# Where side jobs of an attention kernel begin, who reads them in its tail, and the order of its first rows

## The chip, the core and the metric

The kernel runs on one NeuronCore of a Trainium2 chip. The metric is the device time of one execution in microseconds (us). PE is TensorE, DVE is VectorE, ACT is ScalarE, POOL is GpSimd and SP is SyncE, which here issues most of the DMAs.

## What is computed

The input x has 4 batches of 1024 rows of 128 features. All of it is float32. Two blocks with a layer norm ahead follow each other, both with 16 heads of 8 features.

```python
x = x + attention(layernorm(x))      # softmax over (q k / sqrt(8)) * tril(k=-1), then @ Wr + br
x = x + ffn(layernorm(x))
# ffn(y): q, k from rotary(y), v from y; causal attention, out projection
#   x1 = layer_norm(y + attn_out)
#   gates = softmax(x1 @ gate_w.T + gate_b), the two largest of 8 experts
#   moe = sum of the two experts' outputs (x1 @ expert_w + expert_b) times their gates
#   return layer_norm(x1 + moe)
```

In the first attention the scores above the diagonal are multiplied by zero ahead of the softmax, so they still count in its sum. In the second they are minus infinity.

## The kernel before

**Slots and sets.** There are 8 attentions, 4 batches of 2 blocks, and each is a *slot* (`SLOTS`). Their order mixes the blocks: (0,0), (0,1), (1,0), (0,2), (1,1), (0,3), (1,2), (1,3). A slot has 8 passes (half of the queries, 4 heads), and a pass goes through *sets* of key tiles (`SETS`), 3 for the first half of the queries and 7 for the second. So a slot has 40 sets and all slots have 320. A full set has two *units*. A unit is one ACTIVATE, the exponential over 128x1024 scores (line 1275). The last set of each pass is a half set with one unit. There are 576 units.

**What the engines do for a set g.** PE writes the scores (`scores_set`, line 1101). It may begin when the first exponential of set g-1 has been taken, since there are three pairs of PSUM banks for scores. ACT takes the exponentials, POOL masks the diagonal tiles (line 1351), and PE multiplies the probabilities of set g-3 with the values (`value_group`, line 1130, `LAG` is 3). Once a pass, ACT copies the sums out of PSUM (`evacuate`, line 1218).

**Side jobs.** All other work of PE (projections, transposes, the gates, two jobs e0 and e1 for each tile of 128 rows with the eight experts) is cut into *jobs*, 219 in all, of which 178 stand beside the sets. Each writes one bank, `side`, and DVE reads it out before the next may begin. For one attention of the second block, work `p2` makes q, k and v ahead of it, and work `p3` is what follows it. `p1` makes them for the first block. Everything else that is not attention is a *turn* of DVE, POOL, ACT or SP.

**Who sets the order.** `schedule()` runs while the kernel is built. It keeps a clock for each engine and writes down what each engine does at each of 640 points, two to a set. Point 2g lies between the scores of set g and the values of set g-3, and point 2g+1 after those values. Every job and turn has a latest time, from `ends` and `UNIT_TIME`. Before the change a job may begin when `credit` is above zero. That is an account which fills evenly with what is left to do, and from which each job takes its PE time, so jobs are spread evenly whatever PE and ACT are at. What is left after set 319 stands in `AFTER`, the tail. Each engine works its list in order and waits on semaphores. In the tail the six score banks serve as job banks as well.

**The tail.** The last half of the rows is `LAST_HALF`, rows 512 to 1023 of batch 3 in the second block. After its attention come `num` (transposes of the sums), `att`, `att_turned`, `out`, `stats`, `root`, `centre`, `scale`, `x1T`, `gate`, `exp`, `pick0` to `pick3`, `GT`, `bias`, the four tiles' `e0`, `e1` and `moe`, then `stats2`, `root2`, `centre2`, `scale2` and `store`. For a tile DVE multiplies the two banks of e0 and e1 with the gates (`prod`, line 1391) and adds the two (`psum`), and POOL adds the rest (`moe`, lines 1332 to 1334).

**The start.** `BEFORE_TURNS` is written by hand. DVE first works on `pairs`, a small bound made from the weights, for which PE waits for `first_weights_in`. Five loads count on that semaphore, `bv` the last of them.

## Time and profile before

| what | value |
|---|---|
| median of 3 runs | 813.0 us (808.07 to 815.91) |
| the profiled execution | 811.53 us |
| its span, first to last instruction | 809.8 us |
| mean granted clock of TensorE | 0.938 |
| first exponential begins | 32.04 us |
| last store issued, landed | 806.51 us, 809.32 us |
| PE, ACT, DVE, POOL busy | 660.4, 632.5, 409.4, 323.6 us |

The profile is of one execution, and its span is 1.7 us shorter than that execution's time. The kernel has three stretches: a start of 32 us without exponentials, the 320 sets, and a tail after the last exponential, which begins at 745.66 us and takes 1.11 us. An idle time in the rows is that of the engine just before the instruction, and the arrow names what ended it.

### The profile page before, as it was taken

The page shows a single profiled execution, that of the slowest core. Times are in us where ns is not written, and L with a number is a line of the kernel's source. Part 1 is how long each engine was busy: PE and PEld are TensorE (multiplying, and loading weights), DVE is VectorE, ACT ScalarE, POOL GpSimd, SP SyncE. Part 2 cuts the span into 40 slices and gives each one's busy share as a digit, 9 for nine tenths or more (in the row PEclk, how much of TensorE's full clock was granted, in tenths as well). Part 3 has the DMA queues.
Part 4 walks back from the last instruction along what each step waited for, and adds up shares of the span by engine and source line. Part 5 has one row for each costly group of instructions (what it writes and reads, how often), then busy time and mean ns, then how long its engine had stood idle before and what let it go on. Part 6 is the DMA issues. An engine that isn't in the chain of part 4 may idle for free. (4 is left out here: it accounts for less than half of the span.)

```text
span 809.8 us, 15314 instructions
## 1 busy us (share of the span) xinstructions
PE 660.4 (82%) x5560; PEld 246.2 (30%) x5560; DVE 409.4 (51%) x1115; ACT 632.5 (78%) x665; POOL 323.6 (40%) x635
## 2 busy tenths in 40 slices
PE   3589888898798879879878889899888889799643
PEld 2324223332233223223223323323322323223321
DVE  4365452355354542564444634553734535545876
ACT  1389998899799987889979899798898997977000
POOL 3162245332532433534643436414743346224323
PEclk9699999999899998999989999889999999999857
DMA  5866467363566343433365334241554434410000
GB/s 136 272 203 207 146 218 227 99 203 134 185 231 188 134 141 98 133 93 118 121 210 159 132 106 147 81 132 49 170 193 145 158 96 121 119 53 2 26 26 15
DMA packets 76992, 109.78 MB, mean 136 GB/s; under 512 B 13784, under 2 KB 28256, under 8 KB 76896
## 3 DMA queue, kind: packets, MB, share of 16 engines
q1 hardware_dynamic: 73232, 107.85, 42.0%
q10 hardware_dynamic: 3664, 0.77, 0.5%
q8 instruction: 46, 0.75, 0.4%
q14 instruction: 50, 0.41, 0.2%
HBM read 60.91 MB, written 47.68 MB: 134 GB/s over the span
## 5 line engine op out<-in xcount | busy, mean ns | idle before, releaser
L1275 ACT ACTIVATE probs<-scores,shift 128x1024 f32<-128x1024 f32 x576 | 600.7, 1124 | 101.6 <-PE scores L1101 96.1
L1351 POOL TENSOR_SCALAR_AFFINE_SELECT probs<-probs 128x256 f32<-128x256 f32 (+1 forms) x448 | 197.9, 460 | 393.6 <-ACT probs L1275 392.5
L1130 PE MATMUL acc<-probs,v 128*9 128x512 f32 (+3 forms) x3072 | 326.5, 514 | 0.9 <-ACT num L1218 0.8
L1101 PE MATMUL scores<-qs,ks 32*128 32x512 f32 (+3 forms) x1536 | 161.2, 435 | 81.0 <-ACT probs L1275 78.9
L1101 PEld LDWEIGHTS scores<-qs,ks 32*128 32x128 f32 x1536 | 72.9, 189 | 282.4 <-ACT probs L1275 200.6
L1130 PEld LDWEIGHTS acc<-probs,v 128*9 128x9 f32 x3072 | 59.0, 101 | 109.8 <-issue 71.7
L1391 DVE TENSOR_TENSOR prod<-side,G 128x512 f32<-128x512 f32 x47 | 32.5, 691 | 85.2 <-PE side L1083 75.0
L1083 PE MATMUL side<-we,x1T 128*128 128x512 f32 x94 | 54.5, 663 | 3.6 <-DVE shift L1521 2.0
L1218 ACT ACTIVATE num<-acc 128x512 f32<-128x512 f32 x64 | 38.3, 599 | 5.8 <-PE scores L1005 3.3
L1332 POOL TENSOR_TENSOR moe<-psum 128x256 f32<-128x256 f32 x32 | 23.9, 747 | 42.6 <-DVE x1b L1391 25.4
L1307 POOL TENSOR_TENSOR rstd<-rstd,expo 128x4 f32<-128x4 f32 x32 | 33.8, 1056 | 2.7
L1240 ACT ACTIVATE ga<-gl 128x32 f32<-128x32 f32 x8 | 2.0, 246 | 31.5 <-DVE gl L1391 31.5
L1391 DVE TENSOR_TENSOR psum<-prod 128x512 f32<-128x512 f32 x32 | 23.4, 732 | 4.7 <-POOL y L1334 0.6
L1424 DVE COPY xT<-side 128x512 f32<-128x512 f32 x22 | 15.1, 686 | 18.4 <-PE side L956 18.4
L1436 DVE TENSOR_SCALAR part<-side,binqk 128x512 fp32r<-128x512 f32 x16 | 12.0, 749 | 23.0 <-PE side L962 21.3
L1083 PEld LDWEIGHTS side<-we,x1T 128*128 128x128 f32 x94 | 14.3, 191 | 28.0 <-issue 12.4
L1306 POOL TENSOR_SCALAR rstd<-mv 128x4 f32<-128x4 f32 x32 | 8.0, 250 | 33.5 <-DVE mv L1402 33.5
L1406 DVE TENSOR_SCALAR xn<-xrow,mv,rstd 128x128 f32<-128x128 f32 x32 | 11.2, 410 | 19.0 <-POOL rstd L1307 19.0
L1083 PE MATMUL scores<-we,x1T 128*128 128x512 f32 x34 | 20.3, 713 | 0.0
L1436 DVE TENSOR_SCALAR part<-side,bqk 128x512 fp32r<-128x512 f32 x12 | 9.0, 751 | 20.5 <-PE side L962 20.5
L1399 DVE BATCH_NORM_STATS2 stats<-xrow 128x6 f32<-128x128 f32 x64 | 13.8, 276 | 10.6 <-DMA xrow<-in_x 7.5
L962 PE MATMUL side<-xT,win 128*128 128x512 f32 x32 | 18.0, 645 | 0.0
(171 smaller groups left out, 604.3 us busy)
## 6 DMA issues: line engine op xcount, KB each, us to landing
ks<-k_dram SPq DMA_DIRECT2D x96, 256.0 KB, 4.0
q_dram<-part SPq DMA_DIRECT2D x64, 256.0 KB, 3.1
qs<-q_dram SPq DMA_DIRECT2D x64, 256.0 KB, 3.1
num_dram<-num SPq DMA_DIRECT2D x60, 256.0 KB, 3.3
k_dram<-part SPq DMA_DIRECT2D x32, 256.0 KB, 3.6
xrow<-in_x SPq DMA_DIRECT2D x16, 256.0 KB, 4.3
nat<-num_dram SPq DMA_DIRECT2D x15, 256.0 KB
rdenb<-rden_dram SPq DMA_DIRECT2D x15, 256.0 KB
```

Of the source, the lines that this page charges most:

```text
L962: signal(pe.matmul(out[:, :], w[:, int(name == "k"), :], xT[a][:, a or j, :], start=True, stop=True), last)
L1083: signal(pe.matmul(out[:, :], x1T[i // TH][:, i % TH, :], we[:, first:first + HALF], start=True, stop=True), last)
L1101: ins = pe.matmul(scores[:, pair(g, h // 2), h % 2, col:col + w], ks[u][r, kt // TH, (kt % TH) * P:(kt % TH + 1) * P], qs[u][r, q0:q0 + w] ...
L1130: ins = pe.matmul(acc[h * VW:h * VW + VC, q0:q0 + w], v9[V_OF[k]][:, kt, :, HG * hg + h], src, start=(s == 0), stop=last, skip_group_check ...
L1218: act.activation(num[gp % 2][:, :], acc[:, :], ACT.Copy).then_inc(acc_read, 1)
L1275: act.activation(dst, src, ACT.Exp, bias=shift[:, column(k):column(k) + 1], scale=SCALE).then_inc(probs_raw, 1)
L1307: pool.tensor_tensor(r, r, expo[:, 0:1].broadcast_to(list(r.shape)), ALU.pow).then_inc(root_ready[w], 1)
L1332: link(pool.tensor_tensor(moe[:, :, :], psum4[:, i % 2, 0:2, :], psum4[:, i % 2, 2:4, :], ALU.add))
L1351: ins = pool.affine_select(out=blocks, in_=blocks, compare_op=ALU.is_ge, fill=0.0, base=a - 1, pattern=[[0, blocks.shape[1]], [1, P]], cha ...
L1391: return dve.tensor_tensor(out, in0, in1, op)
L1424: freeing(dve.tensor_copy(xT[a][:, int(name == "rT") if a else j, :], written(job)))
L1436: link(dve.tensor_scalar(pt[:, c, 0, :], src, bias[:, c:c + 1], None, ALU.add))
```

## The change

There are four parts. All of them change the lists of the engines, three by the plan and one by new instructions.

**Where jobs begin.** `credit` is gone. A job may begin when, by the build's clocks, PE would be at most `LATE` (0.5) behind the earliest time of its next scores after the job. Jobs of `p2` are free of that rule, and so is any job whose latest time has passed. The clocks' numbers change, and `UNIT_TIME` goes from 1.25 to 1.15.

**The tail's plan.** It now orders by the longest way left (`left`) and plans PE and DVE apart. 37 jobs are in the tail and 29 were.

**Who reads the tail's banks.** In the tail ACT multiplies the products of all e1 jobs and of the e0 jobs of other halves than the last, 19 of 23, with four ACTIVATEs of 128x128 each. It also copies `x1T` and `GT` (2 each, where their job is in the tail) and `att_turned`. DVE no longer does these, but waits at their place in its list and counts the bank free (`read_by_act`). Products of the tail go to the buffers of `probs`. The last half has its own tiles for y, x1 and x2 (`y_of`, `x1_of`, `x2_of`), in `xrow0` and `xrow`, so it need not wait for the halves before it.

**The start.** The rows' statistics come ahead of `pairs`, `xT` ahead of `bound`, `bv` has its own semaphore, ACT makes the first part of k for both halves (`K_BY_ACT`), and ACT issues the two DMAs of the first k instead of SP.

```diff
+def by_act(x):
+    return x[2] in ("e1", "x1T", "GT", "att_turned") or (x[2] == "e0" and (x[1], x[3] // TH) != LAST_HALF[1:])
...
-BEFORE_TURNS = ([("p0", 0, "pairs", 0), ("p1", 0, "stats", 0), ("p1", 0, "stats", 1), ("p1", 0, "root", 0), ("p1", 0, "root", 1),
-                 ("p1", 0, "rows", 0), ("p0", 0, "bound", 0), ("p1", 0, "rows", 1), ("p1", 0, "xT", 0), ("p0", 0, "roots", 0),
+BEFORE_TURNS = ([("p1", 0, "stats", 0), ("p1", 0, "root", 0), ("p1", 0, "stats", 1), ("p1", 0, "root", 1), ("p0", 0, "pairs", 0),
+                 ("p1", 0, "rows", 0), ("p1", 0, "xT", 0), ("p0", 0, "bound", 0), ("p1", 0, "rows", 1), ("p0", 0, "roots", 0),
...
-UNIT_TIME = 1.25
+UNIT_TIME = 1.15
+LATE = 0.5
...
-        credit = min(credit + side_left / (NPOINT - p), 1.5)
         room = p % 2 or len(units) > 1
-        if room and open_job is None and banks[-1] <= t and credit > 0 and p + 4 < NPOINT:
-            x = next((x for x in pending if x[2] in PIECES and ready(x, t, p)), None)
+        if room and open_job is None and banks[-1] <= t and p + 4 < NPOINT:
+            ahead = t + (0.49 * len(UNITS_OF[g - LAG]) if p % 2 == 0 and g >= LAG else 0.0) - exps[FIRST_UNIT[g]] - 0.1
+            x = next((x for x in pending if x[2] in PIECES and ready(x, t, p)
+                      and (x[0] == "p2" or ahead + JOB_TIMES[x[2]][0] * JOB_TIMES[x[2]][1] <= LATE or late(x) < t)), None)
...
+        if clock["DVE"] <= t:
+            x = next((x for x in pending if x[2] not in PIECES and turn_time(x)[0] == "DVE" and ready(x, t, NPOINT)), None)
+            if begun and begun[0][1] <= t and ready(begun[0][0], t, NPOINT) and (x is None or left(begun[0][0]) > left(x)):
+                x, _end = begun.pop(0)
...
-        n_first = len(FIRST) + 1
+        n_first = len(FIRST)
...
+        def k_out(engine, a, b, j):
+            engine.wait_ge(side_free, done((("p1", "p2")[a], b, "k", j)))
+            use = part_count(a, b, j)
+            for d in range(2):
+                engine.dma_start(k_d[a][b, j, :, :, d].rearrange("h e s -> (h e) s"),
+                                 part[use % 2][:, 1, d, :].bitcast(F32)).then_inc(part_out[use % 2], 16)
...
+                if (work, b, name, i) in K_BY_ACT:
+                    act.wait_ge(side_done, done((work, b, name, i)))
+                    act.activation(part[part_count(0, b, i) % 2][:, 1, 0, :], bank_of((work, b, name, i)), ACT.Identity, bias=bqk[:, 1:2]).then_inc(act_parts, 1)
+                if (work, b, name, i) == ("p1", 0, "parts_out", 0):
+                    k_out(act, 0, b, i)
...
+                if job in BY_ACT:
+                    act.wait_ge(side_done, done(job))
+                    src = bank_of(job)
+                    if name in ("e0", "e1"):
+                        act.wait_ge(G_ready, 2 * b + i // TH + 1)
+                        act.wait_ge(products_ready, b * T + i - 1)
+                        c = int(name[1])
+                        for e in range(NE // 2):
+                            ins = act.activation(products(b, i, c)[:, e, :], src[:, e * D:(e + 1) * D], ACT.Copy, scale=G[i // TH][:, i % TH, NE // 2 * c + e:NE // 2 * c + e + 1])
+                    else:
+                        dst = {"x1T": x1T[i], "GT": GT, "att_turned": attT[1]}[name]
+                        rows = NE if name == "GT" else P
+                        ins = act.activation(dst[:, :, :].rearrange("p t s -> p (t s)"), src[0:rows, :], ACT.Copy)
+                    ins.then_inc(act_read, 1)
...
+            def read_by_act(job):
+                dve.wait_ge(act_read, BY_ACT_ORDER.index(job) + 1)
+                dve.wait_ge(side_free, done(job) - 1)
+                dve.sem_inc(side_free, 1)
```

**The order on PE in the last slot.** `scores<-qs,ks` are scores, `acc<-probs,v` values, `side<-we,x1T` an e0 or e1 job, `side<-be,GT` the `bias` job. Before, from the scores of set 286, a full one with a job at both of its points:

```order
L1101 MATMUL scores<-qs,ks 128x512 x4
L1083 MATMUL side<-we,x1T 128x512
L1130 MATMUL acc<-probs,v 9x512 x4
L1083 MATMUL side<-we,x1T 128x512
L1101 MATMUL scores<-qs,ks 128x384 x4
L1101 MATMUL scores<-qs,ks 128x128 x4
L1130 MATMUL acc<-probs,v 9x384 x4
L1130 MATMUL acc<-probs,v 9x128 x4
L1078 MATMUL side<-be,GT 128x128 x4
```

After, in the same stretch, from the scores of set 288, a half one (128x256), to that of set 291:

```order
L1183 MATMUL scores<-qs,ks 128x256 x4
L1212 MATMUL acc<-probs,v 9x256 x4
L1165 MATMUL side<-we,x1T 128x512
L1183 MATMUL scores<-qs,ks 128x512 x4
L1212 MATMUL acc<-probs,v 9x512 x4
L1183 MATMUL scores<-qs,ks 128x384 x4
L1183 MATMUL scores<-qs,ks 128x128 x4
L1212 MATMUL acc<-probs,v 9x384 x4
L1212 MATMUL acc<-probs,v 9x128 x4
L1183 MATMUL scores<-qs,ks 128x256 x4
L1212 MATMUL acc<-probs,v 9x256 x4
L1165 MATMUL side<-we,x1T 128x512
```

The two jobs that stood on both sides of one set's values now stand in different sets, and they stand behind the values of half sets.

**The order on DVE at the start.** Before:

```order
L1461 COPY square<-scores 9x9
L1391 TENSOR_TENSOR square<-square,scores 9x9
L1464 TENSOR_REDUCE total<-square 9x1
L1399 BN_STATS stats<-xrow 128x6 x4
L1402 BN_AGGR mv<-stats 128x2 x4
L1399 BN_STATS stats<-xrow 128x6 x4
L1402 BN_AGGR mv<-stats 128x2 x4
L1406 TENSOR_SCALAR xrow<-xrow,mv,rstd 128x128 x4
L1467 TENSOR_SCALAR c2w<-scores 128x1
L1406 TENSOR_SCALAR xrow<-xrow,mv,rstd 128x128 x4
L1424 COPY xT<-scores 128x512
```

After:

```order
L1509 BN_STATS stats<-xrow 128x6 x4
L1512 BN_AGGR mv<-stats 128x2 x4
L1509 BN_STATS stats<-xrow 128x6 x4
L1512 BN_AGGR mv<-stats 128x2 x4
L1576 COPY square<-scores 9x9
L1501 TENSOR_TENSOR square<-square,scores 9x9
L1579 TENSOR_REDUCE total<-square 9x1
L1516 TENSOR_SCALAR xrow<-xrow,mv,rstd 128x128 x4
L1534 COPY xT<-scores 128x512
L1582 TENSOR_SCALAR c2w<-scores 128x1
L1516 TENSOR_SCALAR xrow<-xrow,mv,rstd 128x128 x4
```

The statistics now come ahead of the three instructions on `square` and `total`, and the copy of `xT` ahead of the second rows.

**The order on DVE at the head of the tail.** Before, from the first product there:

```order
L1391 TENSOR_TENSOR prod<-scores,G 128x512
L1530 COPY tot<-scores 128x4x36
L1719 TENSOR_REDUCE gsum<-gb 128x4
L1391 TENSOR_TENSOR G<-gb,gsum 128x32
L1391 TENSOR_TENSOR G<-G,iota 128x32
L1722 TENSOR_REDUCE gidx<-G 128x4
L1391 TENSOR_TENSOR G<-iota,gidx 128x32
L1391 TENSOR_TENSOR prod<-scores,G 128x512
L1391 TENSOR_TENSOR psum<-prod 128x512
L1530 COPY tot<-scores 128x4x36
```

After, from the sum of the first tile, whose products are one of DVE's own (`prod`) and one of ACT's (`probs`):

```order
L1501 TENSOR_TENSOR psum<-prod,probs 128x512
L1501 TENSOR_TENSOR y<-scores,xr 128x512
L1501 TENSOR_TENSOR x1b<-scores,x 128x512
L1509 BN_STATS stats<-y 128x6 x4
L1512 BN_AGGR mv<-stats 128x2 x4
L1645 COPY tot<-scores 128x4x36
L1520 SCALAR_TENSOR_TENSOR y<-y,mv,l1w 128x128 x4
L1645 COPY tot<-scores 128x4x36
L1501 TENSOR_TENSOR psum<-probs 128x512
L1526 SCALAR_TENSOR_TENSOR x<-y,rstd,l1b 128x128 x4
L1664 RECIPROCAL rden<-tot 128x64
```

The products are gone from DVE's list, and the statistics, `centre` and `scale` of the half before the last have come into it. On ACT, where nothing stood after the last `num` but one `ga`, now stands:

```order
L1378 ACTIVATE probs<-scores,shift 128x1024 x8
L1300 ACTIVATE num<-acc 128x512
L1335 ACTIVATE probs<-scores,G 128x128 x8
L1335 ACTIVATE probs<-side,G 128x128 x4
L1335 ACTIVATE probs<-scores,G 128x128 x4
L1339 ACTIVATE x1T<-scores 128x512
L1335 ACTIVATE probs<-scores,G 128x128 x4
L1339 ACTIVATE attT<-scores 128x512
L1335 ACTIVATE probs<-scores,G 128x128 x4
L1343 ACTIVATE ga<-gl 128x32
L1335 ACTIVATE probs<-side,G 128x128 x4
```

Four 128x128 rows are one product, and it is these that DVE's list waits for.

## Rows read from the trace of the kernel before

**Rows 1.** The page: span, busy shares, exponentials (idle), a DMA issue (landing).

```profile
span 809.8 us, 15314 instructions
...
PE 660.4 (82%) x5560; PEld 246.2 (30%) x5560; DVE 409.4 (51%) x1115; ACT 632.5 (78%) x665; POOL 323.6 (40%) x635
...
L1275 ACT ACTIVATE probs<-scores,shift 128x1024 f32<-128x1024 f32 x576 | 600.7, 1124 | 101.6 <-PE scores L1101 96.1
...
xrow<-in_x SPq DMA_DIRECT2D x16, 256.0 KB, 4.3
```

**Rows 2.** Busy time by stretch, columns named in the first line.

```profile
core 0: us, PE busy (x) PEld busy (x) DVE busy (x) ACT busy (x) POOL busy (x), PEclk, DMA share, GB/s
...
657.00:746.00 89.00, 78.22 (x652) 27.49 (x648) 42.68 (x116) 75.88 (x80) 38.54 (x79) 0.96 0.28 83
746.00:810.00 64.00, 32.75 (x132) 16.22 (x121) 48.43 (x141) 1.60 (x3) 22.11 (x39) 0.75 0.07 21
```

**Rows 3.** All waits: total us, times, longest us.

```profile
ACT probs L1275 <- PE scores L1101: 96.1, 122, 18.7
...
PE scores L1101 <- ACT probs L1275: 78.9, 149, 1.5
```

**Rows 4.** ACT's timeline: start us, us, operation, idle before.

```profile
89.17 2.12 ACT L1275 ACTIVATE probs<-scores,shift 128x1024 f32<-128x1024 f32 x2 [0.70 <-PE scores L1101]
91.69 3.12 ACT L1275 ACTIVATE probs<-scores,shift 128x1024 f32<-128x1024 f32 x3 [0.40 <-PE scores L1101]
...
419.03 1.11 ACT L1275 ACTIVATE probs<-scores,shift 128x1024 f32<-128x1024 f32 x1 [3.65 <-PE scores L1101]
```

**Rows 5.** Timeline of all engines at a set with two jobs.

```profile
668.79 1.12 PE L1083 MATMUL side<-we,x1T 128*128 128x512 f32 x2
669.85 0.51 PE L1101 MATMUL scores<-qs,ks 32*128 32x384 f32 x8
...
670.29 1.06 PE L1130 MATMUL acc<-probs,v 128*9 128x384 f32 x16
670.41 3.32 ACT L1275 ACTIVATE probs<-scores,shift 128x1024 f32<-128x1024 f32 x3 [1.41 <-PE scores L1101]
...
674.42 2.12 ACT L1275 ACTIVATE probs<-scores,shift 128x1024 f32<-128x1024 f32 x2 [0.21 <-PE scores L1101]
```

**Rows 6.** Timeline of the start.

```profile
0.79 1.01 SPq L892 DMA_DIRECT2D xrow<-in_x  x2
...
7.99 0.21 PE L1029 MATMUL scores<-pairs 8*9 8x9 f32 x2 [7.99 <-DMA bv<-in_bv]
...
8.70 0.85 DVE L1399 BATCH_NORM_STATS2 stats<-xrow 128x6 f32<-128x128 f32 x4
...
11.53 1.11 DVE L1406 TENSOR_SCALAR xrow<-xrow,mv,rstd 128x128 f32<-128x128 f32 x4 [0.40 <-POOL rstd L1307]
...
18.45 0.75 DVE L1436 TENSOR_SCALAR part<-scores,bqk 128x512 fp32r<-128x512 f32 x1 [0.17 <-PE scores L962]
...
28.99 2.07 PE L1043 MATMUL side<-later,v 128*128 128x128 f32 x8 [1.54 <-DVE sfx L1600]
```

**Rows 7.** Groups by line in 746 to 810 us: busy, mean ns.

```profile
L1391 DVE TENSOR_TENSOR prod<-scores,G 128x512 f32<-128x512 f32 x17 | 11.5, 684 | 2.3 <-PE scores L1083 2.0
L1391 DVE TENSOR_TENSOR psum<-prod 128x512 f32<-128x512 f32 x9 | 6.6, 737 | 1.2
```

**Rows 8.** Timeline of the tail.

```profile
745.01 3.46 PE L1130 MATMUL acc<-probs,v 128*9 128x512 f32 x40
...
749.62 0.69 DVE L1391 TENSOR_TENSOR prod<-scores,G 128x512 f32<-128x512 f32 x1 [1.16 <-PE scores L1083]
750.06 0.60 ACT L1218 ACTIVATE num<-acc 128x512 f32<-128x512 f32 x1 [3.29 <-PE scores L1005]
...
782.13 0.23 ACT L1240 ACTIVATE ga<-gl 128x32 f32<-128x32 f32 x1 [31.47 <-DVE gl L1391]
...
806.51 0.39 SPq L889 DMA_DIRECT2D out_rows<-y  x1
```

182 lines of the change are left out of this document (124 added, 58 removed).

## The prediction

> **What bounds the kernel now.** I read the page first: span, busy shares and the row of the exponentials [rows 1]. The reader is to see that neither PE (82%) nor ACT (78%) is full, and that ACT was idle for 101.6 us ahead of exponentials. The windows come next [rows 2]. In the last eighth of the sets ACT is busy for 75.9 of 89 us and PE for 78.2. In the tail ACT does 1.6 us in 64, while DVE is busy for 48.4. So DVE and its chain bound the tail, and in the sets PE and ACT hold each other up: ACT waited 122 times for scores, 96.1 us in all, 18.7 of them the start, and PE's scores waited 149 times for ACT, 78.9 us [rows 3].
>
> ACT's timeline shows two kinds of wait [rows 4]. After a half set it is nearly always there, at 89.17 us with 0.70 us, because the scores of the next set may only begin once the half set's one exponential is done. After a full set PE has the second exponential as cover. A third is rare and long, 3.65 us at 419.03 us, in the set behind a `norm` job for which PE waited in order. At a set with two jobs [rows 5] PE does its second job until 669.85 us, the scores come after it, and ACT has sat idle for 1.41 us. At 674.42 us, behind one job, it is 0.21 us.
>
> I put each of ACT's idle times beside the jobs that the build has in the set before it. They add up to 101.6 - 18.7 = 83 us, to the tenth [rows 1, 3]:
> - half sets without a job, 36: 17.9 us, 0.50 each; with a job, 27: 21.6 us, 0.80 each
> - full sets without a job, 113: 2.6 us, 0.02 each
> - full sets with one p2 job, 53: 13.2 us, 0.25 each
> - full sets with one p1 or p3 job, 82: 22.3 us, 0.27 each; with two jobs, 8: 5.4 us, 0.67 each
>
> About 32 us of it (63 half sets at 0.50) is the sets' own structure, and no order of jobs takes it away. Some 51 us is what jobs cost.
>
> **The sets under the new rule.** The lists of the changed kernel have 170 jobs beside the sets and had 178. No set has two. By the same classes there are 21 half sets without a job, 42 with one, 128 full sets without, 59 with a p2 job and 69 with a p1 or p3 job.
> - Half sets: 21 x 0.50 + 42 x 0.80 = 44.1 us, against 39.5. That is 4.6 us more. Behind a half set nothing covers a late PE, and the rule treats it like a full one.
> - Full sets without a job: 128 x 0.02 = 2.6 us, as before.
> - p2 jobs are free of the rule: 59 x 0.25 = 14.8 us. The `norm` that cost 3.65 us stood 7 points behind its k and now stands 14. I take half of that wait and half of a second like it off: 11.3 us, against 13.2, so 1.9 less.
> - p1 and p3 jobs: these begin where PE is on time, so I price them between nothing and the 0.21 us of the single job in [rows 5], at 0.16, since some are transposes half as long. 69 x 0.16 = 11.0 us, against 22.3 + 5.4 = 27.7. So 16.7 less.
>
> That is 14.0 us less idle. ACT also gains a little when it doesn't stop: three exponentials without a stop took 3.12 us and two took 2.12 [rows 4], so the next begins 1.00 us on although one lasts 1.11. For some 20 stops fewer that is 2 us. **Sets: -16 us.** Bounds: with every class at its old mean, 69 x 0.27 for p1 and p3 and 14.8 for p2, it is 44.1 + 2.6 + 14.8 + 18.6 = 80.1, a gain of 3; take 1 at the upper end, for lengths within a class. With p1 and p3 jobs at nothing and no long waits, it is about 31 us.
>
> **The start.** DVE's statistics began at 8.70 us, behind `pairs`, which waited for bv until 7.99 us. The rows were issued at 0.79 us, and such a load lands in 4.3 us [rows 1, 6], so they lay there by about 5.6 us. Now the statistics come first, and `pairs` waits for one load less. By then the roots are ready, and the first rows begin about when `pairs` is through, at 8.3 us where it was 11.53 [rows 6]: 3.2 us earlier. Behind that, ACT takes one instruction of 0.75 us off DVE for each half's k. The first is covered, since DVE waited for PE there (0.17 us) [rows 6]; the second is worth about 0.8 us. The first scores waited for PE to finish the `suffix` job begun at 28.99 us [rows 6], which hangs on DVE's last v, so the gain arrives. **Start: -4 us**, between -1.5 (loads land late) and -5. That ACT now waits for k and issues two DMAs costs nothing, since it has no exponential until the first scores.
>
> **The tail.** DVE's busy time was 48.4 us [rows 2]. Off its list go 14 of 18 products at 0.684 us (9.6), 4 copies of about 0.68 (2.7) and one `num`. On it come 3 more sums at 0.737 us (2.2) [rows 7], and, by the same sizes, statistics, `centre` and `scale` of the half before the last (3.5), its gate and first pick (1.8), and out, bias and pre (2.1). The sum is about 45 us with eight more jobs than before.
>
> What DVE waits for is the other half of it. Its list now begins with a sum that needs ACT's first product. The values end at 748.5 us, PE's first job a microsecond later, then ACT needs its product, so DVE begins at about 750.8 us where its first product began at 749.62 [rows 8]; before that it had picks to do, and now nothing, some 2.5 us lost. A product by ACT is not in the trace. Its bounds come from a 128x32 ACTIVATE of 0.23 us and a 128x512 one of 0.60 [rows 8]: about 0.32 for 128x128, four of them 1.27 us end to end or 0.93 overlapped like exponentials. I take 1.1, near the middle. On ACT 19 products are 21 us and 5 copies 3, in 60 us, so ACT is no bound. But DVE waits in order. Following the list, I find four places where ACT has only just been given the bank (two products behind the `x1T` of each half, one after the last pick, the first `GT`), 4.3 us together. At the end stay about 5.7 us of moe, statistics, root and store. DVE idles for 4.0 us at the head (746.8 to 750.8), and I add 4 us for the other waits on PE and POOL: 45 + 4.0 + 4.3 + 5.7 + 4 = 63 us, as long as now (746.8 to 809.8). **Tail: 0 us**, between -8 (the own tiles and the longest-way order close all gaps but the ends) and +10 (DVE waits at every second product).
>
> The Trainium skill, "ScalarE: Activation LUTs", section "What ACT_TABLE_LOAD costs", gives an ACTIVATE with immediates 186 ns and 0.833 ns for each column, 93 ns more with a pointer for the scale, and 93 ns of overlap back to back. For 512 columns that is 0.61 us, which the trace's 0.60 agrees with, and by an estimate from that page a product is 1.27 us. With it the sum would come out 1 to 3 us longer.
>
> **Sum.** -4 - 16 + 0 = -20 us. The profiled execution took 811.53 us, so 791.5. The median of the runs is 1.5 us above it, and I forecast **793 us**.
>
> **Rivals.**
> - *The rule holds fully.* p1 and p3 jobs cost nothing and no `norm` stalls: sets -31, start -4, tail 0: 778 us. For it speaks that full sets in which PE had time to spare cost 0.02 us. Against it: a single 1.06 us job already cost 0.21 us at 674.42 us [rows 5], and the rule lets it begin.
> - *The build's clocks are not the chip's.* The change then doesn't do what it says. Jobs stand elsewhere, but each class keeps its price: sets -1 to -3, start -3, tail 0: 808 us. For it speaks that the clocks know nothing of the stretches at the lower clock (0.96 and 0.75 granted in [rows 2]).
> - *DVE waits for ACT.* The sets gain 16, but the tail loses: each of 19 products held for its full 1.27 us is 24 us of waiting. 45 + 24 + 5.7 = 75 us, 12 more than now: 805 us. The skill's same page, "Rules for kernel authors", says to use VectorE and not ScalarE for a multiply, which speaks for this rival. The trace can only say that DVE did a product in 0.684 us [rows 7].
> - *Backlog, slower.* PE falls behind over neighbouring sets. 66 full sets have a job beside themselves and beside the one before, and 60 had. They cost 0.19 us each. If delays add up there as they do in sets with two jobs (0.67 each), the idle time is 66 x 0.67 + 62 x 0.25 + 44.1 + 2.6 = 106 us where it was 83: +23, less 4 at the start: 832 us. It decides from about 0.4 us each. Against it: PE still waited for ACT for 78.9 us [rows 3], so it catches up.
>
> **How the numbers follow.** My forecast has 0.55 (its own range 783 to 804), the full rule 0.15, DVE's waits 0.10, the foreign clocks 0.13, the backlog 0.07. A measurement here tells about 1% from no change, 805 to 821 us. Faster by over 1%: 0.54 + 0.15 + 0.05 + 0.03 = 0.77. Within: 0.01 + 0.05 + 0.10 = 0.16. Slower: 0.07. The range leaves out the backlog and the far ends of the others: 774 to 810 us.
>
> **What the profile would show.** First exponential at about 28 us (32.04). From it to the last some 699 us (714.7 to its end). ACT's idle time for scores, without the start, under 72 us, and no set with 1.4 us behind two jobs. A new wait of DVE for ACT in the tail of 5 to 10 us, DVE busy about 45 us there, and last exponential to end about 63 us. I am wrong if waits behind half sets grow well over 0.8 us, if a p2 chain is late at the head of a slot, or if ACT's products take much over 1.3 us.

## The result, and the profile after

The changed kernel took 799.4 us (median of 4 runs, 796.04 to 802.52), the kernel before 811.1 beside it. The ratio is 0.985 [0.981, 0.989]: faster by 1.5%. The forecast was 793, inside 774 to 810, so the sign and the range hold and the forecast was 6 us too low. The profiled execution took 796.04 us with a span of 794.3, which is 15.5 less than [rows 1].

I cut every trace at the start of the first exponential and at the end of the last, and call what lies between them the sets and what follows the tail.

| stretch, us | before | after | change | forecast |
|---|---|---|---|---|
| to the first exponential | 32.04 | 27.24 | -4.8 | -4 |
| the sets | 714.7 | 693.0 | -21.7 | -16 |
| the tail | 63.0 | 74.05 | +11.0 | 0 |
| span | 809.8 | 794.3 | -15.5 | -20 |

The page of the kernel after, against [rows 1] and [rows 7]:

```profile
span 794.3 us, 15432 instructions
...
PE 651.4 (82%) x5560; PEld 245.9 (31%) x5560; DVE 394.4 (50%) x1089; ACT 654.6 (82%) x748; POOL 321.0 (40%) x635
...
L1378 ACT ACTIVATE probs<-scores,shift 128x1024 f32<-128x1024 f32 x576 | 596.5, 1125 | 70.0 <-PE scores L1183 64.4
```

ACT's idle time ahead of exponentials fell from 101.6 to 70.0 us. 7.1 of the 70.0 is the start, so the sets hold 62.8, where they held 82.9. All waits of the kernel after, against [rows 3] (total us, times, longest us):

```profile
PE scores L1183 <- ACT probs L1378: 72.9, 152, 1.5
...
ACT probs L1378 <- PE scores L1183: 64.4, 93, 7.1
...
DVE psum L1501 <- DVEq L1498: 12.7, 8, 7.7
...
PE side L1059 <- POOL sq L1418: 6.2, 4, 2.4
...
DVE xr L1501 <- DVEq L1498: 2.5, 1, 2.5
...
DVE gl L1501 <- DVEq L1498: 1.4, 1, 1.4
```

ACT waited 93 times where it waited 122 times. New are the waits behind L1498, the line in which DVE waits for a bank that ACT reads.

Busy time by stretch, for the sets and the tail. The first two rows are the kernel before, the last two the kernel after:

```profile
core 0: us, PE busy (x) PEld busy (x) DVE busy (x) ACT busy (x) POOL busy (x), PEclk, DMA share, GB/s
32.04:746.77 714.73, 613.47 (x5384) 220.19 (x5384) 344.38 (x925) 629.24 (x658) 295.32 (x584) 0.96 0.45 144
746.77:809.80 63.03, 31.98 (x124) 16.21 (x120) 47.74 (x139) 0.83 (x2) 21.34 (x37) 0.74 0.07 22
...
27.24:720.26 693.02, 594.78 (x5350) 213.93 (x5354) 330.82 (x892) 625.92 (x657) 286.71 (x573) 0.97 0.47 149
720.26:794.31 74.05, 42.84 (x158) 23.15 (x150) 47.79 (x148) 24.86 (x85) 27.15 (x47) 0.76 0.08 22
```

In the tail DVE is busy for 47.8 us, as it was before (47.7), although ACT now does 24.9 us there. DVE was rid of work and was given as much again, and it idles for 26.3 us where it idled for 15.3.

**The start**, against [rows 6]:

```profile
4.17 0.87 DVE L1509 BATCH_NORM_STATS2 stats<-xrow 128x6 f32<-128x128 f32 x4 [2.71 <-DMA xrow<-in_x]
...
6.61 0.21 PE L1111 MATMUL scores<-pairs 8*9 8x9 f32 x2 [6.61 <-DMA bqk<-in_bqk]
...
7.37 1.10 DVE L1516 TENSOR_SCALAR xrow<-xrow,mv,rstd 128x128 f32<-128x128 f32 x4
...
10.42 3.78 PE L1044 MATMUL scores<-xT,wqkv 128*128 128x512 f32 x4 [0.27 <-DVE xT L1534]
...
13.25 0.20 ACT L1317 ACTIVATE clw<-c2w 128x1 f32<-128x1 f32 x1 [7.01 <-issue]
...
13.72 0.17 DVE L1587 TENSOR_SCALAR shift<-ccw 128x4 f32<-128x4 f32 x1 [2.02 <-ACT ccw L1318]
...
27.24 2.12 ACT L1378 ACTIVATE probs<-scores,shift 128x1024 f32<-128x1024 f32 x2 [7.10 <-PE scores L1183]
```

The first rows begin at 7.37 us, 4.16 earlier than at 11.53, since the first load lay there by 4.17 and `pairs` waits for one load less. The forecast had 8.3 us, from a load that lands at 5.6. DVE then stands for 2.02 us behind ACT's `ccw`, which ACT made only at 13.48 us, having issued loads until 13.20. PE's four matmuls from 10.42 us on are the products of q and then of k. By the single records the second ends at 12.49 us, but DVE reads q at 14.54; in the kernel before it read q right behind PE (16.74 after 16.70). So some of the start's gain may lie unused here. No run tests it.

**The tail's head**, against [rows 8]:

```profile
721.76 1.13 PE L1165 MATMUL scores<-we,x1T 128*128 128x512 f32 x2
...
722.93 1.14 ACT L1335 ACTIVATE probs<-scores,G 128x128 f32<-128x128 f32 x4 [0.43 <-PE scores L1165]
...
724.39 0.69 DVE L1501 TENSOR_TENSOR psum<-prod,probs 128x512 f32<-128x512 f32 x1 [7.75 <-DVEq L1498]
```

ACT's product, which no trace had shown, takes 1.14 us for its four ACTIVATEs; 1.1 was assumed. The head is as forecast: DVE waits from the end of the exponentials at 720.26 us to 724.39, 4.1 us against 4.0. The Trainium skill, "ScalarE: Activation LUTs", section "What ACT_TABLE_LOAD costs", led to an estimate of 1.27; the measured 1.14 decides.

**Further on in the tail**, the longest wait behind the head. It is one of the forecast's four places, the product behind `x1T` of the half before the last, and the forecast had 4.3 us for all four:

```profile
730.46 2.14 DVE L1526 SCALAR_TENSOR_TENSOR x<-y,rstd,l1b 128x128 f32<-128x128 f32 x4
...
732.75 1.09 PE L1141 MATMUL scores<-ident,x 128*128 128x128 f32 x4 [4.29 <-DVE x L1526]
...
733.63 1.92 PE L1165 MATMUL scores<-we,x1T 128*128 128x512 f32 x2
...
735.58 1.14 ACT L1335 ACTIVATE probs<-scores,G 128x128 f32<-128x128 f32 x4 [1.11 <-PE scores L1165]
...
736.95 0.69 DVE L1501 TENSOR_TENSOR psum<-probs 128x512 f32<-128x512 f32 x1 [2.83 <-DVEq L1498]
```

DVE's `x` ends at 732.60 us, PE had waited for it for 4.29 and then takes 1.92 for an e1 job. The clock granted from 733.6 to 735.6 us is 0.50, the lower level; where it is 1.00, such a job takes 1.02 to 1.13. ACT takes 1.14, and DVE, whose next instruction is the sum of just this product, has waited for 2.83. ACT is far from full, at 24.9 of 74 us. It is the way from DVE over PE and ACT back to DVE that costs this wait.

### The profile page after: what moved, and what is told of

It is laid out like the page before. It is cut to its first block and busy times, and to the rows that moved or that the text cites. A ratio compares the mean times of both kernels' runs of the same rounds, so it can differ in the third digit from the quotient of the medians.

```text
span 794.3 us, 15432 instructions
## 1 busy us (share of the span) xinstructions
PE 651.4 (82%) x5560; PEld 245.9 (31%) x5560; DVE 394.4 (50%) x1089; ACT 654.6 (82%) x748; POOL 321.0 (40%) x635
## 5 line engine op out<-in xcount | busy, mean ns | idle before, releaser
L1454 POOL TENSOR_SCALAR_AFFINE_SELECT probs<-probs 128x256 f32<-128x256 f32 (+1 forms) x448 | 195.7, 453 | 366.1 <-ACT probs L1378 365.5
L1212 PE MATMUL acc<-probs,v 128*9 128x512 f32 (+3 forms) x3072 | 318.9, 503 | 4.1 <-ACT num L1300 4.1
L1183 PE MATMUL scores<-qs,ks 32*128 32x512 f32 (+3 forms) x1536 | 159.1, 428 | 74.9 <-ACT probs L1378 72.9
L1501 DVE TENSOR_TENSOR prod<-side,G 128x512 f32<-128x512 f32 x41 | 28.3, 691 | 84.3 <-PE side L1165 84.2
L1335 ACT ACTIVATE probs<-scores,G 128x128 f32<-128x128 f32 x60 | 16.7, 392 | 20.7 <-PE scores L1165 9.4
L1534 DVE COPY xT<-side 128x512 f32<-128x512 f32 x22 | 15.2, 690 | 19.9 <-PE side L1038 17.1
L1165 PE MATMUL scores<-we,x1T 128*128 128x512 f32 x36 | 22.5, 739 | 0.0
L1549 DVE TENSOR_SCALAR part<-side,bqk 128x512 fp32r<-128x512 f32 x12 | 9.0, 751 | 27.1 <-PE side L1044 27.0
L1509 DVE BATCH_NORM_STATS2 stats<-xrow 128x6 f32<-128x128 f32 x72 | 15.6, 278 | 13.2 <-DMA xrow<-in_x 11.2
L1165 PEld LDWEIGHTS side<-we,x1T 128*128 128x128 f32 x92 | 14.5, 194 | 22.7 <-issue 18.8
L1436 POOL TENSOR_TENSOR moe<-moe 128x128 f32<-128x128 f32 x32 | 15.6, 487 | 2.5
L1501 DVE TENSOR_TENSOR psum<-prod 128x512 f32<-128x512 f32 x20 | 15.3, 765 | 2.6
```

The lines of the kernel that those rows point to most:

```text
L1165: signal(pe.matmul(out[:, :], x1T[i // TH][:, i % TH, :], we[:, first:first + HALF], start=True, stop=True), last)
L1183: ins = pe.matmul(scores[:, pair(g, h // 2), h % 2, col:col + w], ks[u][r, kt // TH, (kt % TH) * P:(kt % TH + 1) * P], qs[u][r, q0:q0 + w] ...
L1212: ins = pe.matmul(acc[h * VW:h * VW + VC, q0:q0 + w], v9[V_OF[k]][:, kt, :, HG * hg + h], src, start=(s == 0), stop=last, skip_group_check ...
L1335: ins = act.activation(products(b, i, c)[:, e, :], src[:, e * D:(e + 1) * D], ACT.Copy, scale=G[i // TH][:, i % TH, NE // 2 * c + e:NE // ...
L1454: ins = pool.affine_select(out=blocks, in_=blocks, compare_op=ALU.is_ge, fill=0.0, base=a - 1, pattern=[[0, blocks.shape[1]], [1, P]], cha ...
L1501: return dve.tensor_tensor(out, in0, in1, op)
```

## The experiments

All are compared with the kernel before on the same chip; its medians beside them were 809.3 to 809.7 us. The last four columns are in us and of one profile each. All tails below are from the end of the last exponential to the end of the span.

| run | median, us (runs) | ratio [95%] | first exp. | sets | tail (jobs) | DVE busy in the tail |
|---|---|---|---|---|---|---|
| start_only | 807.5 (10) | 0.997 [0.994, 0.9995] | 27.5 | 717.2 | 63.5 (29) | 47.8 |
| rule_only | 809.6 (10) | 1.000 [0.997, 1.0025] | 32.5 | 694.4 | 79.0 (36) | 60.1 |
| tail_dve | 805.0 (10) | 0.994 [0.990, 0.997] | 27.5 | 697.6 | 79.4 (37) | 62.1 |
| tail_copies | 803.6 (10) | 0.994 [0.991, 0.9965] | 27.3 | 692.5 | 79.0 (37) | 59.3 |
| old_rule | 801.2 (4) | 0.987 [0.981, 0.993] | 26.3 | 715.1 | 57.9 (29) | 36.3 |
| last_slot | 794.6 (4) | 0.982 [0.976, 0.987] | 27.1 | 699.6 | 64.2 (32) | 38.9 |
| last_plan | 792.0 (4) | 0.9775 [0.971, 0.984] | 27.4 | 697.6 | 64.9 (32) | 38.7 |
| last_fill | 801.7 (4) | 0.990 [0.983, 0.9965] | 27.3 | 696.9 | 72.6 (32) | 38.7 |
| last_half | 813.5 (10) | 1.005 [1.002, 1.009] | 27.4 | 719.7 | 63.5 (32) | 38.9 |
| chain_sq | 794.2 (4) | 0.983 [0.978, 0.987] | 29.6 | 695.9 | 66.5 (31) | 38.8 |
| p2_ruled | 798.1 (4) | 0.988 [0.983, 0.992] | 27.8 | 701.9 | 64.9 (32) | 39.1 |

Runs whose lists beside the sets are the same word for word show how much the sets scatter from one profile to the next: 714.7, 717.2 and 715.1 us (before, start_only, old_rule), 693.0, 697.6 and 692.5 (after, tail_dve, tail_copies), and 699.6, 697.6 and 696.9 (last_slot, last_plan, last_fill). A difference of less than 5 us between the sets of two single profiles shows nothing by itself.

### The parts alone: start_only, rule_only, tail_dve

start_only is the kernel before with the changed start and nothing else:

```diff
-BEFORE_TURNS = ([("p0", 0, "pairs", 0), ("p1", 0, "stats", 0), ("p1", 0, "stats", 1), ...
+BEFORE_TURNS = ([("p1", 0, "stats", 0), ("p1", 0, "root", 0), ("p1", 0, "stats", 1), ...
+K_BY_ACT = [x[:4] for x in BEFORE if x[2] == "k" and x[5]]
```

> The kernel before with the change of the start alone: order of the first rows, own semaphore for bv, ACT makes the first part of k and issues the first k's two DMAs. My prediction's term for the start was -4 us, and the profile after shows the first exponential 4.8 us earlier. If that is all of its effect, this kernel is 4 to 5 us faster than before (ratio 0.994), its first exponential is at 27 to 28 us, and sets and tail are as before, 714.7 and 63.0 us. The rival is that the later stretches give it back (a transfer that then collides in slot 0): then the first exponential is early, and the sets are longer by about the same.

The first exponential came 4.6 us earlier (27.46 for 32.04), and the sets took 2.5 us longer, so the span fell by 1.65 us and the median by 0.3%. 4 to 5 us were expected. Part of the gain is given back in the first sets: the first ten take 24.8 us where they took 23.1, and 26.3 in old_rule, whose first exponential is at 26.3 us. So the eleventh set begins 2.9 and 2.6 us earlier than before.

rule_only is the kernel before with the new rule, its clocks and `UNIT_TIME`; the start, the tail's plan and its readers are the old ones:

```diff
-            clock["PE"] += 0.26 * len(units)
+            clock["PE"] += 0.22 * len(units)
...
-        if room and open_job is None and banks[-1] <= t and credit > 0 and p + 4 < NPOINT:
-            x = next((x for x in pending if x[2] in PIECES and ready(x, t, p)), None)
+            ahead = t + (0.49 * len(UNITS_OF[g - LAG]) if p % 2 == 0 and g >= LAG else 0.0) - exps[FIRST_UNIT[g]] - 0.1
+            x = next((x for x in pending if x[2] in PIECES and ready(x, t, p)
+                      and (x[0] == "p2" or ahead + JOB_TIMES[x[2]][0] * JOB_TIMES[x[2]][1] <= LATE or late(x) < t)), None)
```

> The kernel before with the new rule of where jobs begin, its clocks and UNIT_TIME, and nothing else: the old start and the old plan of the tail, in which DVE reads every bank (36 jobs in the tail). Sets of 691 to 696 us are expected, since the rule is the only thing that changes them (after: 692.9). The tail tells two theories apart. Theory W (waits): the tail after is 74.1 us because DVE waits in its list for ACT's products, so with DVE reading it is at most 69 us (63.0 and some 0.8 us for each of seven jobs more). Theory J (jobs): it is long because more work was pushed out of the sets into a stretch in which nothing covers it, at 1.4 us a job, whoever reads: 72 to 76 us.

Sets and tail, columns as above:

```profile
32.45:726.86 694.41, 597.10 (x5352) 214.98 (x5356) 332.95 (x893) 626.18 (x657) 287.68 (x573) 0.97 0.46 147
726.86:805.85 78.99, 42.70 (x156) 22.09 (x148) 60.07 (x170) 1.06 (x4) 27.50 (x47) 0.73 0.07 21
```

The sets gain 20.3 us and the tail loses 16.0, more than either theory had (at most 69 us, and 72 to 76). The median is that of before. By itself the rule moves time from the sets into the tail.

tail_dve is the changed kernel with DVE as the only reader of the tail:

```diff
 def by_act(x):
-    return x[2] in ("e1", "x1T", "GT", "att_turned") or (x[2] == "e0" and (x[1], x[3] // TH) != LAST_HALF[1:])
+    return False
```

> The changed kernel with DVE making all products and copies of the tail, as before; its plan, own tiles, start and rule stay, and the sets are the same word for word. DVE gets back some 16.5 us of work and loses 17.9 us of waits for ACT. Theory W (waits): much of that wait was not needed, so the tail is 68 us or less. Theory J (jobs): the tail is 73 to 80 us, and giving work to ACT was right or of no effect.

```profile
725.03:804.40 79.37, 43.53 (x158) 24.23 (x150) 62.06 (x172) 1.05 (x3) 27.76 (x47) 0.74 0.07 21
```

The tail is 5.3 us longer than with ACT as a reader (79.4 and 74.05), with DVE busy for 14.3 us more. So reading by ACT is worth its place in the tail, though only some two fifths of what it takes off DVE arrive at the end. The own tiles and the new plan for the tail show little here: 79.4 us with 37 jobs, against 79.0 with 36 in rule_only, which has neither. No run has them alone.

### The other half of the square: old_rule and tail_copies

old_rule is the changed kernel with the old rule and its numbers, so that the jobs beside the sets are those of the kernel before:

```diff
+        credit = min(credit + side_left / (NPOINT - p), 1.5)
-        if room and open_job is None and banks[-1] <= t and p + 4 < NPOINT:
+        if room and open_job is None and banks[-1] <= t and credit > 0 and p + 4 < NPOINT:
```

> The changed kernel with the old rule for jobs beside the sets (credit, the old clocks and UNIT_TIME), so that the lists beside the sets are those of the kernel before; start, plan of the tail, own tiles and ACT's reading are the new ones. 29 jobs in the tail. It tells what the tail's own parts are worth without more jobs. If ACT's reading takes 5 us off a tail, as between the last run's tail (79.5 us with DVE) and the changed kernel's (74.1), the tail is 57 to 59 us and sets 715 us: 801 to 804 us, no slower than 1% above the changed kernel, so most of the gain needs no new rule. If the reading helps only when the tail is crowded, the tail stays at 61 to 63 us and the kernel at 806 to 808.

```profile
26.28:741.36 715.08, 612.59 (x5384) 220.52 (x5384) 346.33 (x924) 628.67 (x658) 294.32 (x584) 0.96 0.45 144
741.36:799.29 57.93, 32.84 (x124) 17.21 (x120) 36.34 (x121) 18.54 (x62) 21.38 (x37) 0.74 0.09 24
```

This closes the square. The jobs in the tail cost the same whoever reads:

| tail, us | 29 jobs | 36 or 37 jobs | difference |
|---|---|---|---|
| DVE reads, old start and plan (before, rule_only) | 63.0 | 79.0 | +16.0 |
| DVE reads, new start, new plan on the right only (start_only, tail_dve) | 63.5 | 79.4 | +15.9 |
| ACT reads too (old_rule, after) | 57.9 | 74.05 | +16.1 |

That is 2 us for each of eight jobs (seven in the first row). Most of it is work of DVE that comes with the jobs: of the 16 us, DVE's busy time is 12.3, 14.2 and 11.5, and its waits are the other 3.6, 1.7 and 4.7. The rule's gain in the sets is 20.3, 19.6 and 22.1 us in the same three rows. ACT's reading is worth 5.3 us with the many jobs and, with own tiles and plan in it, 5.6 with the few. It takes 14.3 and 11.5 us off DVE and brings 9.0 and 6.0 us of waits. So the tail's +11 is 16 for the jobs less 5 for the readers.

old_rule is also the whole change without its rule, and it takes 801.2 us, 0.987 [0.981, 0.993], which the 0.985 [0.981, 0.989] of the changed kernel can't be told from. What gains here are the start and above all ACT's reading, which alone takes the ratio from 0.994 (tail_dve) to 0.985.

tail_copies lets ACT make the copies only:

```diff
-    return x[2] in ("e1", "x1T", "GT", "att_turned") or (x[2] == "e0" and (x[1], x[3] // TH) != LAST_HALF[1:])
+    return x[2] in ("x1T", "GT", "att_turned")
```

> The changed kernel in which ACT makes in the tail only the copies (x1T, GT, att_turned) and DVE all products. The sets and the start are planned as in the changed kernel; 37 jobs stand in the tail. With DVE reading everything the tail took 79.5 us at 62.1 us of DVE's busy time, with ACT reading products and copies 74.1 us at 47.8. Theory P (the products are what DVE is rid of): copies alone take about 3 us of DVE's busy time off and give less than 1.5 us: tail 78 to 79.5, DVE busy 58 to 60 us, time within 0.3% of the run with DVE as the only reader, 803 to 806. Theory C (a product that DVE must wait for is worth little, a copy on ACT lets PE go on): the tail comes to 75 to 76 us with DVE busy for 58 us, and the time to 799 to 801.

Its tail took 79.0 us with DVE busy for 59.3, and its ratio is that of tail_dve. So theory P holds: the copies gave 0.35 us for 2.8 us less of DVE's busy time, and the products gave the other 5.0 for 11.5. Here DVE's long wait is for PE, not for ACT (total us, times, longest us, in the tail):

```profile
DVE probs L1501 <- PE scores L1165: 10.0, 4, 6.3
```

### Jobs back out of the tail: last_slot, last_plan, last_fill

last_slot lets every job of the last slot begin as before the rule, whatever PE's count says:

```diff
-                      and (x[0] == "p2" or ahead + JOB_TIMES[x[2]][0] * JOB_TIMES[x[2]][1] <= LATE or late(x) < t)), None)
+                      and (x[0] == "p2" or g >= SETS_ALL - GB or ahead + JOB_TIMES[x[2]][0] * JOB_TIMES[x[2]][1] <= LATE or late(x) < t)), None)
```

> The changed kernel with one clause more: in the last slot (its 40 sets) every job may begin whenever it is ready, as p2 jobs may. 32 jobs in the tail where there were 37. Theory J: each job that comes back to the sets saves 1.4 us of the tail and costs up to 0.3 us of idle ACT: tail 67 to 69 us, sets 694 to 696, in all 4 to 6 us faster than the changed kernel. Theory W: the tail hangs on the waits, not on the count, so it is 72 to 74 us, and in all the kernel is not faster by more than 1 us.

The tail has 32 jobs and takes 64.2 us, 9.9 less than after; the sets take 6.6 more. The five jobs were expected to save 7 us in the tail at most and to cost 1.5 in the sets, so both terms are larger. Part of the 6.6 is scatter: over the three profiles of each list the sets take 698.0 us against 694.4, so 3.7 more, or 0.7 for each job. Both the median and the span (790.8) are below those of the changed kernel, though the intervals of the ratios overlap.

last_plan adds the measured price of ACT's product to the tail's plan:

```diff
-                    clock["ACT"] = max(clock["ACT"], t) + (0.9 if x[2] in ("e0", "e1") else 0.6)
+                    clock["ACT"] = max(clock["ACT"], t) + (1.3 if x[2] in ("e0", "e1") else 0.7)
```

> The kernel with all jobs free in the last slot, and the tail planned with what a product by ACT really takes, 1.14 us and its signals: 1.3 for 0.9 in the plan, and 0.7 for 0.6 for a copy. Nothing beside the sets changes. If DVE waits for ACT because the plan puts its turn too early, the tail gets shorter by 2 to 5 us (64.2 before). If they are waits that any order has, since the chain itself runs through ACT, it changes by less than 1 us.

```profile
27.44:724.99 697.55, 603.22 (x5372) 217.65 (x5372) 339.63 (x915) 626.77 (x657) 291.72 (x580) 0.97 0.46 148
724.99:789.88 64.89, 36.91 (x136) 18.69 (x132) 38.74 (x127) 21.17 (x72) 24.07 (x41) 0.75 0.08 21
```

It has the lowest median of all, with 0.9775 [0.971, 0.984] against before; the interval of the changed kernel reaches down to 0.981. The plan's price is not what did it: its tail is 64.9 us where last_slot has 64.2, and the two intervals overlap widely. What both have in their profiles over the changed kernel lies in the five jobs that left the tail: it is 9.9 and 9.2 us shorter, and DVE is busy there for 8.9 and 9.1 us less.

last_fill is last_slot with two matmuls into a bank that nobody reads ahead of each job of the tail, to see what the lower clock costs there:

```diff
+                    if x[2] in PIECES:
+                        for _ in range(FILL):
+                            pe.matmul(acc[:, 0:256], ident[:, :], we[:, 0:256], start=True, stop=True)
```

> The kernel with all jobs free in the last slot, and two matmuls of 128x128 by 128x256 into acc, which nobody reads, ahead of each job of the tail. They are work that isn't needed; the output stays the reference's. In the tail the granted clock is 0.76, and an e job takes PE 1.9 us at the lower level where it takes 1.02 at the higher. If the clock lengthens the tail, fillers that keep PE at work raise it to 0.9 and more and shorten the tail by 3 to 6 us. If PE's jobs are covered by DVE, the tail stays or gets up to 10 us longer by the fillers themselves.

```profile
724.24:796.80 72.56, 55.78 (x264) 39.09 (x260) 38.68 (x127) 22.33 (x73) 24.01 (x41) 0.96 0.07 19
```

The clock granted in the tail rose from 0.77 to 0.96, and the tail became 8.4 us longer than last_slot's. PE is busy for 20.8 us more, and a part of that lies on the path: DVE's first read of the transposed sums came 7.6 us after the last exponential (5.1 in last_slot), since PE reached those transposes behind fillers. The edit also lets PE wait for ACT's last copy of the sums ahead of the tail, which takes 0.8 us of it. The run does not tell what the lower clock costs by itself, only that fillers in the way of jobs do not pay.

### Behind half sets: last_half

The forecast priced a job behind a half set at 0.30 us over an empty one. last_half is last_slot with a limit of 0.1 for those places, which leaves 29 jobs behind half sets where there were 40:

```diff
-... ahead + JOB_TIMES[x[2]][0] * JOB_TIMES[x[2]][1] <= LATE or late(x) < t)), None)
+... ahead + JOB_TIMES[x[2]][0] * JOB_TIMES[x[2]][1] <= (LATE if len(units) > 1 else 0.1) or late(x) < t)), None)
```

> The kernel with all jobs free in the last slot, and LATE at 0.1 for jobs that begin behind a half set's values, where the rule had 0.5. My prediction held that such a job costs 0.3 us, since nothing covers it, and priced it at 0.80 us against 0.50 without; the profile after has 0.54 for p3 jobs there. If the old price is right, 11 fewer of them make it 3 us faster. If the measured one is right, it is within 1 us of the kernel with the last slot free, or slower, since those jobs now stand in full sets.

It is 20 us slower in the sets than last_slot, and ACT's idle time there is 86.7 us where it was 68.7. One expectation had 3 us faster and the other no change or slower, and neither had that size. The half sets hold 47.2 us where they held 41.5, and full sets with a p1 or p3 job 15.6 where they held 7.3. By the build's schedule 25 p1 and p3 jobs now begin where PE is too late for the rule, only because their latest time has passed, and the sets behind them idle for 9.2 us; there were 6 of them in last_slot, with 1.9. Another 4.2 us are one set in which a `norm` and a `top` came together:

```profile
458.42 0.47 PE L1059 MATMUL side<-headsum,sq 128*128 128x16 bf16 x12 [2.41 <-POOL sq L1418]
...
460.65 0.90 PE L1066 MATMUL side<-ident,nrm 128*128 128x128 f32 x3
461.49 0.80 PE L1183 MATMUL scores<-qs,ks 32*128 32x512 f32 x4
...
462.34 1.11 ACT L1378 ACTIVATE probs<-scores,shift 128x1024 f32<-128x1024 f32 x1 [4.17 <-PE scores L1183]
```

Places behind half sets are worth more than they cost. In the kernel after, the 23 half sets with a p3 job idle for 0.54 us each, and the 21 without a job for 0.52. The 19 with a p1 or p2 job idle for 0.93.

### The waits that are left: chain_sq and p2_ruled

After the change, 59 full sets with a p2 job hold 16.1 us of ACT's idle time, more than all other full sets together (5.8). One of the longest is at a `norm`, in the kernel after:

```profile
275.57 0.47 PE L1059 MATMUL side<-headsum,sq 128*128 128x16 bf16 x12 [2.44 <-POOL sq L1418]
...
275.96 1.90 PE L1212 MATMUL acc<-probs,v 128*9 128x512 f32 x8
...
277.80 0.80 PE L1183 MATMUL scores<-qs,ks 32*128 32x512 f32 x4
...
278.65 1.11 ACT L1378 ACTIVATE probs<-scores,shift 128x1024 f32<-128x1024 f32 x1 [3.35 <-PE scores L1183]
```

ACT waits for 3.35 us though PE waited for only 2.44. Behind PE's wait the granted clock is 0.50 (276.0 to 277.8 us), and the eight matmuls of the values take 1.90 us where the same eight take 1.06 at a granted clock of 1.00 (561.41 us). So this wait of PE cost ACT more than its own length, and the `norm` wait of [rows 4] looks the same, with eight of them in 1.90 us from 416.35 us on.

chain_sq plans 5.0 us instead of 3.3 for POOL's squares, in last_plan, so that `norm` stands further behind its k:

```diff
-"sq": ("POOL", 3.3, 0.2),
+"sq": ("POOL", 5.0, 0.2),
```

> The best version so far (every job of the last slot begins freely, and the tail's plan counts 1.3 us for a product by ACT) with one number more: the plan's time of POOL's squares (sq) goes from 3.3 to 5.0 us, so that the norm jobs of p2 stand further behind their k. In the changed kernel the full sets with a p2 job cost 16.1 us of ACT's idle time, 0.27 each, and the longest had PE waiting for a norm behind the squares, an xT behind the rows or a k behind DVE. Theory N (the squares are what PE waits for): the p2 class falls to about 10 us, the longest wait of a norm to under 1 us, and the sets from 697.5 to about 692: 786 to 788 us. Theory M (the waits only move to another step of the chain, or the next slot's head gets late since the chain is longer): the p2 class stays between 14 and 19 us, sets 696 to 700, time within 3 us of 792. The tail has 31 jobs instead of 32, which is worth -2 us at most in either.

The class of full sets with a p2 job did fall, from 15.2 to 7.1 us (with 49 such sets instead of 59), as theory N says, and half sets with one from 11.8 to 7.2. But the other classes took most of it: full sets with a p1 or p3 job went from 6.3 to 14.5 us, and six sets now have two jobs and cost 5.6. By the schedule 13 p1 and p3 jobs begin past their latest time, with 7.1 us behind them, where 6 did with 1.9. The sets gain 1.6 us, less than the scatter, and the time is within 3 us of last_plan: theory M, though its class was to stay. The tail was to be 2 us shorter at most for one job less and was 1.6 longer (66.5 us). A new wait of 3.33 us is at a k of p1, for which PE had to wait 2.33 us until DVE had read out a gate.

p2_ruled puts the p2 jobs under the rule too, in last_plan:

```diff
-                      and (x[0] == "p2" or g >= SETS_ALL - GB or
+                      and (g >= SETS_ALL - GB or
```

> The same best version with the jobs of p2 under the rule as well: they too begin only where the build's count has PE at most 0.5 us late. It asks whether the full sets with a p2 job cost 0.27 us each because PE has no time to spare there (theory T) or because PE waits within them for another engine (theory N). Theory T: the class falls from about 16 us to under 8, and the sets to about 690, time 784 to 787. Theory N: the class keeps 13 to 17 us, and the chain, which now ends only a point or two ahead of its slot, adds waits at slot heads: sets 698 to 703, time 792 to 798.

The class fell to 6.6 us, which is what theory T says of it, and the sets (701.9 us) and the time (798.1) rose as in theory N, as did the waits at slot heads: at two of them the `shift` that ends the chain was late, with 2.71 and 2.83 us for ACT (total us, times, longest us):

```profile
ACT probs L1378 <- DVE shift L1636: 5.5, 2, 2.8
```

last_plan has no such wait. Full sets with a p3 job rose from 5.6 to 15.4 us, the half sets with a p2 job from 11.8 to 14.6 (the 5.5 are in these), and one set with two jobs alone cost 3.9. A p2 job held back pushes others over their latest times, and there the rule does not hold: 12 p1 and p3 jobs begin so, with 9.2 us behind them, where 6 did with 1.9. So leaving the p2 jobs free is right here, and the price of a class is not the price of its job.

## Why the prediction was right, and where it was not

**The start.** Right, -4.8 against -4, by the steps named. The rows began at 7.37 us where 8.3 was worked out. "The gain arrives" was said of the first scores and counted in full for the end, and there less arrives: start_only has 1.65 us of span and 0.3% of the median.

**The sets.** The mechanism was right and the size too small, -21.7 against -16. ACT's idle time went from 82.9 to 62.8 us, against 69.0 by the forecast's classes:

| class (sets) | forecast, us | measured, us |
|---|---|---|
| half sets, all 63 | 44.1 | 40.9 |
| full, no job (128) | 2.6 | 1.8 |
| full, p2 job (59) | 11.3 | 16.1 |
| full, p1 or p3 job (69) | 11.0 | 4.0 |

Two terms were mis-sized. A p1 or p3 job was priced at 0.16 us and cost 0.06: the rule does what it says, nearly fully, and the single job of [rows 5] with its 0.21 us was not the typical one. The price of 0.80 behind a half set was the mean of a class in which rare waits of 3 to 4 us sit (one of 3.20 among the 27 of the kernel before, 3.96 and 3.36 in old_rule), and not that of a p3 job, which cost 0.02 over an empty place. For p1 and p2 jobs there it was too low, 0.80 against 0.93. The p2 term erred the other way: I took two `norm` waits off, and new ones of 3.44 and 3.35 us came at other places. Beyond the idle time the sets gained 1.6 us, and I had 2.

**The tail.** This term failed, +11.0 against 0. By its own parts:

| part of the tail, us | forecast | measured |
|---|---|---|
| DVE busy | 45 | 47.8 |
| head, before DVE's first sum | 4.0 | 4.1 |
| DVE behind ACT | 4.3 | 10.1 |
| end, and other waits | 5.7 + 4 | 12.0 |

The step that failed is "I find four places where ACT has only just been given the bank, 4.3 us together". At these places DVE waited for 2.83 and 1.43 us (the products behind `x1T` of the two halves) and for 0.75 at the first `GT`, the product after the last pick included: 5.0 together, so their price was about right. But there were nine more such waits after the head, 5.1 us together, 2.54 of them at one place, where DVE's next work had to wait for the product of e0 of the last tile of the half before the last. The other waits and the end took 2.3 us more than counted, and DVE's busy time 2.8 more. The eight more jobs were not left out: what they cost DVE in busy time, 11.5 us of their 16, is in the forecast's 45. What was too small is the waiting that comes with the jobs and with the readers: DVE idled for 15.3 us before and for 26.3 after, where the forecast has 18.0. The pairs of runs say where the 11.0 come from, in either order: 6.0 from ACT's reading and then 4.7 from the jobs (start_only, old_rule, after), or 1.7 from the jobs and then 9.0 from the reading (start_only, tail_dve, after). The granted clock of the tail was 0.74 before and 0.76 after, so it did not lengthen the tail.

**Luck.** That the time fell into the range is in part luck. The sets gained 5.7 us more than forecast and the tail lost 11.0 more, and the two errors have opposite signs. With the sets as forecast and this tail the time would have been 805 us, which the prediction itself calls hard to tell from no change. And what carries the measured gain is not what the forecast built on: it had 16 of its 20 us from the rule, and without the rule the kernel is as fast within the intervals.

**The rivals.** "DVE waits for ACT" had the right place and the wrong reason. It held each of 19 products for its full 1.27 us, 24 us in all; DVE waited 10.1, and ACT's reading is a gain of 5 us and no loss. tail_dve and tail_copies have the products on DVE, and their tails are 5 us longer, since DVE bounded the tail and ACT had nothing to do. The Trainium skill, "ScalarE: Activation LUTs", section "Rules for kernel authors", says to use VectorE for a multiply, for its speed in bf16; here all is float32, and in this tail the measurement speaks against it. "The rule holds fully" came true nearly for p1 and p3 jobs in full sets (0.06 us each), but a `norm` still stalls. The build's clocks are near enough to the chip's for that 0.06, where jobs placed without the rule cost 0.27. There is no backlog: 49 full sets with a p3 job cost 3.3 us in all.

**What stays open.** The rule by itself is worth 4 to 5 us in single spans (before to rule_only 4.0, start_only to tail_dve 3.7, old_rule to after 5.0) but 0.0 to 0.3% in medians, each time inside the intervals, so its worth in this form is not shown. That the versions with fewer jobs in the tail (0.9775 to 0.983) beat the changed kernel is likely by their profiles and not shown by the intervals. What the lower clock costs in the tail is not shown either. And three to seven waits of over 2 us stay in the sets in all of after, last_plan, chain_sq and p2_ruled; whether some order has none of them was not settled.

## What to carry to other kernels

A rule that lets filler work begin only when there is time to spare also decides how much is left over. Price the rest at what it costs where it ends up, here 2 us a job in the tail against some 0.7 us beside the last sets, and loosen the rule over the last stretch. A rule with a way out for late jobs loses there what it gains elsewhere, so count how many jobs take that way. The mean idle time of a class of places is not the price of what stands there: look for the few long waits in it before you multiply. When work is handed from the bound engine to an idle one but the order of both stays fixed, count the round trip and not the busy time: of 14.3 us taken off DVE, 5.3 arrived.

## What was not expected of the hardware

- The granted clock of the tail was 0.72 to 0.77 in every version but the one with fillers (0.96), and in one and the same tail an e0 or e1 job took 1.92 us where the granted clock was 0.50 and 1.02 where it was 1.00.
- Four ACTIVATEs of 128x128 with a pointer as scale, out of PSUM, took 1.14 us end to end, at 0.39 us for one alone (L1335, x60, mean 392 ns): so 0.25 us from one to the next.
- The first exponential came between 26.3 and 29.6 us in the eleven versions with the new start. In chain_sq (29.6) PE took 3.65 us for the second half's four q and k products, after 1.98 us of waiting, at a granted clock of 0.54, and in the kernel after 1.96 us, after 1.48, at 1.00, for the same order.
